# The first layer's feed-forward stage one slot later in a slot-ordered two-layer transformer kernel

## The chip, the cores and the metric

The kernel runs on one core of a Trainium2 chip. The metric is the device time of one execution in microseconds (us). The time before is the median of three runs.

## The reference

Two pre-norm transformer layers act on x of shape (8, 256, 128), 16 heads of 8 features, all in float32:

```python
x = x + attn0(norm(x))   # RoPE, causal; two softmaxes, gated mix, @ Wo.T
x = x + relu(norm(x) @ W1 + b1) @ W2 + b2          # 128 -> 512 -> 128
x = x + attn1(norm(x)*g + b)  # biases, full softmax
x = x + (silu(n @ Wg.T) * (n @ Wu.T)) @ Wd.T       # n = norm(x), 128 -> 384 -> 128
```

## The kernel before

**Phases and slots.** There are 16 phases, i = 0 to 15: first the eight batches of layer 0, then the eight of layer 1. Each phase has 16 slots, one for each head. In slot s, TensorE (PE) first makes the plain scores of head s of the *next* phase (`scores(i + 1, s)`, lines 947 to 951), then the scores of head s of *this* phase with the maximum already subtracted (`shifted(i, s)`, lines 974 to 978). VectorE (DVE) takes the row maxima of the first (lines 774 to 779), ScalarE (ACT) the exponential of the second (line 615). In layer 0 GpSimd (POOL) sets the masked part of two heads' probabilities to zero in each odd slot (`cut`, lines 486 and 489). In slots 6, 10 and 14, and in slot 2 of the next phase (slot 1 behind a phase of layer 1), PE multiplies four heads' probabilities with V (`pv`, line 1000).

**Rings.** Shifted scores alternate between two PSUM banks, so that `shifted(g)` waits for the exponential of slot g - 2. The plain scores have three banks: slot g waits for the maximum of slot g - 3. `pv` for slots 0 to 3 waits for the cuts of slots 1 and 3.

**Everything else rides in the slots.** The dictionary `STEP` says for each step of a batch in which phase (counted from the batch's own) and slot it is issued; `due(L, name, i, s)` is asked in each slot by each engine's program, which is written out in order. So `"xT1": (1, 15)` is issued one phase after the batch's own, in slot 15. An engine's instructions run in exactly that order: a step that waits holds up all behind it.

**The steps around the change**, for batch b of layer 0, are: the output projection is added to x and its statistics taken on DVE (`add_wo`, lines 795 and 710 to 714, slot 11 of phase b + 1); POOL normalises (`norm1`, lines 436 to 443, slot 12); PE transposes the result (`xT1`, line 897) and ACT copies it out (line 660); PE makes the first two blocks of hidden features (`h0`, line 1030), ACT their ReLUs (`relu0`, `relu1`, line 629); then `h1`, `relu2`, `relu3`; then both halves of the second product (`fa` and `f`, line 1043, which sum in one bank); then DVE adds it to x (`add_f`, line 795). `bn2` (the next statistics, slot 13 of phase b + 2) and `norm2` (slot 2 of phase b + 3, POOL) follow.

**The other work in those slots.** Slot 0: PE projects layer 1's V (`v1`, line 1061) and transposes the negated maxima of slots 8 to 15 of the phase at hand (`mr1`, line 957), which needs the maximum made in slot 15 of the phase before. ACT copies both (lines 647, 619). Slot 1: ACT casts (`hi1`, line 674). Slot 4: `oT0` (line 1009), slot 5: `norm_o` (lines 786, 788). POOL: `xb` in slot 4 (line 527), `zg` in slot 6 (line 510); DVE: `z` in slot 7 (line 819); PE: `zT` (line 1016) and `mr0` (line 957) in slot 9, `wo` (line 1022) and `xT2` (line 897) in slot 10.

**Banks.** `xT1`, `h0`, `h1`, `mr0` with `zT`, and `wo` use bank 7 one after the other; each waits until the one before it is emptied. `f`, `xT2`, `qk1`, `mr1` and `oT0` use bank 6. The order of uses is computed from `STEP` by `bank_uses`.

**DMA.** SyncE's queue carries the loads of the stacked operands, the stores to scratch, and the two loads of transposed maxima in each phase (line 369).

Of the kernel before, what the change touches and what calls it, by code (L numbers as in the profile page):

```python
# [40 lines left out]


STEP = ({"oT0": (1, 4), "norm_o": (1, 5), "zg": (1, 6), "z": (1, 7), "zT": (1, 9), "wo": (1, 10), "add_wo": (1, 11),
         "norm1": (1, 12), "xT1": (1, 15), "h0": (2, 1), "relu0": (2, 2), "relu1": (2, 3), "xb": (2, 4), "h1": (2, 5),
         "relu2": (2, 6), "relu3": (2, 7), "fa": (2, 7), "f": (2, 8), "add_f": (2, 9), "bn2": (2, 13), "norm2": (3, 2),
         "xT2": (3, 10), "copy_xT2": (3, 11), "q1": (3, 13), "qk1": (3, 13), "copy_q1": (3, 14), "copy_k1": (3, 14),
         "hi1": (4, 1), "lo1": (4, 10), "v1": (4, 0)},
        {"bv": (0, 10), "oT1": (1, 4), "norm_o": (1, 5), "res": (1, 6), "bn3": (1, 7), "norm3": (1, 8), "xT3": (1, 13), "hi3": (1, 13),
# [1173 lines left out]
```

## Time and profile before

| | |
|---|---|
| Median of three runs | 309.39 us (309.39 to 310.2) |
| The profiled execution's own time | 311.73 us |
| Its span in the profile | 310.0 us |
| Busy, PE / DVE / ACT / POOL | 93% / 80% / 69% / 59% |

The span runs from the first to the last instruction of the core. Busy shares are averages over stages with different limits. The matmuls' ends in the profile are modelled; their starts are used here.

### The profile page before, as it was taken

How to read it: one execution, taken by the hardware profiler on the slowest of the kernel's cores; microseconds unless marked ns; L12 is line 12 of the kernel's file. 1: busy time of each engine (PE TensorE's matmuls, PEld its weight loads, DVE VectorE, ACT ScalarE, POOL GpSimd, SP SyncE). 2: the span in 40 equal slices, each digit the busy share in tenths (PEclk: the TensorE clock that was granted, in tenths of full speed). 3: DMA queues.
4: the chain of work that ended last, by engine and by line, in shares of the span. 5: the costliest groups of instructions: out<-in, count | busy, mean ns of one | idle time of the engine just before them, and what ended most of it. 6: DMA issues, size and time to landing. Idle time of an engine off the chain costs nothing.

```text
span 310.0 us, 8437 instructions
## 1 busy us (share of the span) xinstructions
PE 288.1 (93%) x2833; PEld 206.1 (66%) x2833; DVE 246.9 (80%) x992; ACT 213.2 (69%) x494; POOL 182.2 (59%) x409
## 2 busy tenths in 40 slices
PE   6498898899998999999999999999999999999985
PEld 4375555677676777878687776766666666666564
DVE  7669987687869877686878777679898989896764
ACT  8463784776576868685867768697778767677921
POOL 5475879887785878687778514525455535353210
PEclk9967999999999999999999999999999999999999
DMA  6477436511313121221212010021211101000001
GB/s 188 151 196 176 110 94 178 163 51 56 121 39 103 36 85 54 80 59 41 76 39 60 21 57 26 28 62 29 60 45 52 53 28 44 28 22 1 20 18 35
DMA packets 23691, 21.60 MB, mean 70 GB/s; under 512 B 3712, under 2 KB 20608, under 8 KB 23648
## 3 DMA queue, kind: packets, MB, share of 16 engines
q1 hardware_dynamic: 23648, 21.05, 23.5%
q8 instruction: 23, 0.38, 0.5%
q14 instruction: 20, 0.16, 0.2%
HBM read 13.18 MB, written 7.34 MB: 66 GB/s over the span
## 4 chain that ended last, share of the span: by engine, by line
PE 50%; DVE 22%; POOL 16%; issue 5%; ACT 3%; DMA 2%; SPq 1%; POOLq 0%; ACTq 0%; DVEq 0%
PE bank L1000 11%; DVE NM L779 7%; PE bank L974 5%; PE bank L1043 4%; PE bank L1030 4%; PE bank L950 4%; POOL PB L489 3%; PE bank L951 3%; PE bank L978 3%; POOL XN L443 3%; DVE JUNK L776 3%; PE bank L1089 3%; POOL RS L439 2%; POOL PR L459 2%; DMA xs<-in_x 2%
## 5 line engine op out<-in xcount | busy, mean ns | idle before, releaser
L615 ACT ACTIVATE PB<-bank 128x384 f32<-128x384 f32 (+1 forms) x256 | 134.3, 545 | 47.1 <-PE bank L976 23.6
L779 DVE TENSOR_REDUCE NM<-bank 128x2 f32<-128x512 f32 x128 | 83.8, 683 | 19.7 <-PE bank L951 19.4
L974 PE MATMUL bank<-QS,KS 128*128 128x256 f16 x256 | 69.9, 274 | 3.8 <-ACT PB L615 2.6
L1000 PE MATMUL bank<-PB,VP 128*32 128x256 f32 (+1 forms) x1024 | 61.7, 358 | 0.4 <-ACT PB L615 0.4
L776 DVE CUSTOM_DVE_ANT_0 JUNK<-bank,MSF 128x256 bf16<-128x256 f32 x128 | 53.7, 419 | 0.0
L774 DVE CUSTOM_DVE_ANT_0 JUNK<-bank,MSF 128x128 bf16<-128x128 f32 x128 | 36.3, 284 | 19.5 <-PE bank L948 19.0
L1000 PEld LDWEIGHTS bank<-PB,VP 128*32 128x32 f32 x1024 | 26.8, 109 | 23.2 <-issue 9.7
L489 POOL TENSOR_SCALAR_AFFINE_SELECT PB<-PB 128x512 f32<-128x512 f32 x64 | 41.2, 643 | 0.0
L950 PE MATMUL bank<-KS,QS 96*128 96x256 f16 x128 | 35.2, 275 | 0.4
L948 PE MATMUL bank<-KS,QS 96*128 96x256 f16 x128 | 34.9, 275 | 0.0
L951 PE MATMUL bank<-KS,QS 96*128 96x256 f16 x128 | 34.6, 271 | 0.0
L978 PE MATMUL bank<-QS,KS 128*128 128x256 f16 x128 | 34.3, 271 | 0.0
L974 PEld LDWEIGHTS bank<-QS,KS 128*128 128x128 f16 x256 | 24.6, 96 | 13.6 <-ACT PB L615 10.0
L947 PE MATMUL bank<-KS,QS 96*128 96x128 f16 x128 | 28.7, 225 | 2.6 <-DVE NM L776 2.6
L976 PE MATMUL bank<-QS,KS 128*128 128x128 f16 x128 | 27.8, 217 | 0.0
L486 POOL TENSOR_TENSOR HELD<-EPSC 128x1 f32<-128x1 f32 x64 | 13.1, 205 | 24.5 <-ACT PB L615 24.4
L443 POOL TENSOR_SCALAR XN<-xs,NMN,RS 128x128 f32<-128x128 f32 x54 | 24.5, 463 | 4.8 <-POOL RS L439 4.8
L478 POOL CAST HGL<-HG 128x256 f16<-128x256 f32 x15 | 6.0, 399 | 32.0 <-DVE HG L808 32.0
L897 PE MATMUL bank<-IDF,XN 128*128 128x128 f32 x64 | 13.3, 291 | 7.1 <-DVE XN L721 4.5
L911 PE MATMUL bank<-XT,W 128*128 128x256 f32 x64 | 19.0, 434 | 0.9 <-ACT XT L572 0.6
L439 POOL TENSOR_TENSOR RS<-VE,EPSC 128x2 f32<-128x2 f32 x27 | 19.4, 718 | 0.0
L950 PEld LDWEIGHTS bank<-KS,QS 96*128 96x128 f16 x128 | 12.4, 97 | 10.0 <-DVE NM L779 6.3
(104 smaller groups left out, 590.7 us busy)
## 6 DMA issues: line engine op xcount, KB each, us to landing
scr<-PR SPq DMA_DIRECT2D x16, 256.0 KB, 2.6
QS<-scr SPq DMA_DIRECT2D x16, 128.0 KB, 2.6
QS<-scr SPq DMA_DIRECT2D x32, 64.0 KB, 2.8
KS<-scr SPq DMA_DIRECT2D x32, 64.0 KB, 2.7
KS<-scr SPq DMA_DIRECT2D x16, 128.0 KB, 2.9
scr<-PR SPq DMA_DIRECT2D x16, 128.0 KB, 1.9
out_x<-xs SPq DMA_DIRECT2D x8, 128.0 KB, 2.0
W<-in_w SPq DMA_DIRECT2D x1, 576.0 KB, 4.8
```

The costliest lines, as they stand in the source:

```text
L443: ins = pool.tensor_scalar(XN[n][p][:, t], xs[:, b * TPB + t], NMN[:, n, p, t:t + 1], RS[:, n, p, t:t + 1], ALU.add, ALU.mult)
L489: pool.affine_select(out=pr, in_=pr, compare_op=ALU.is_ge, fill=0.0, base=0, pattern=[[0, 4], [1, P]], channel_multiplier=-1).then_inc(s_c ...
L615: act.activation(PB[:, s % RING, 0:n], scored(i, s)[:, 0:n], ACT.Exp).then_inc(s_e, 1)
L774: dve.tensor_tensor_reduce(JUNK[:, g % 3, 0], o[:, 0:P], MSF[:, 1], -1.0, 3e38, ALU.add, ALU.min, accum_out=m[:, s, 0:1])
L776: dve.tensor_tensor_reduce(JUNK[:, g % 3, 1:3], o[:, P:3 * P].rearrange("q (n k) -> q n k", n=2), MSF[:, :], -1.0, 3e38, ALU.add, ALU.min, ...
L779: dve.tensor_reduce(m[:, s, 0:2], o[:, :].rearrange("q (n k) -> q n k", n=2), AX.X, ALU.max, negate=True).then_inc(s_mx, 1)
L948: ins = pe.matmul(o[:, P:3 * P], q[:, P:2 * P], k[:, :], start=True, stop=True)
L950: pe.matmul(o[:, 0:S], q[:, 0:P], k[:, :], start=True, stop=True)
L951: ins = pe.matmul(o[:, S:2 * S], q[:, P:2 * P], k[:, :], start=True, stop=True)
L974: pe.matmul(o[:, 0:S], k[:, 0:P], q[:, :], start=True, stop=True)
L978: ins = pe.matmul(o[:, S:2 * S], k[:, P:2 * P], q[:, :], start=True, stop=True)
L1000: ins = pe.matmul(o, v, pr, start=(g % 2 == 0 and kt == 0), stop=True, skip_group_check=True)
```

## The change

The transposes of the first layer's FFN input move from slot 15 of phase b + 1 to slot 0 of phase b + 2, and the products, ReLUs, both halves of the output and the add each move one slot on. `xb`, `bn2`, `norm1` and `norm2` stay, and no instruction is added or removed.

```diff
-         "norm1": (1, 12), "xT1": (1, 15), "h0": (2, 1), "relu0": (2, 2), "relu1": (2, 3), "xb": (2, 4), "h1": (2, 5),
-         "relu2": (2, 6), "relu3": (2, 7), "fa": (2, 7), "f": (2, 8), "add_f": (2, 9), "bn2": (2, 13), "norm2": (3, 2),
+         "norm1": (1, 12), "xT1": (2, 0), "h0": (2, 2), "relu0": (2, 3), "relu1": (2, 4), "xb": (2, 4), "h1": (2, 6),
+         "relu2": (2, 7), "relu3": (2, 8), "fa": (2, 8), "f": (2, 9), "add_f": (2, 10), "bn2": (2, 13), "norm2": (3, 2),
```

## Rows read from the trace of the kernel before

**Rows 1.** The page: busy time and share of each engine.

```profile
PE 288.1 (93%) x2833; PEld 206.1 (66%) x2833; DVE 246.9 (80%) x992; ACT 213.2 (69%) x494; POOL 182.2 (59%) x409
```

**Rows 2.** Waits, whole span: waiter, releaser, us in total, times, longest.

```profile
PE bank L897 <- POOL XN L443: 2.1, 5, 0.8
```

**Rows 3.** Stretches: from:to, length, busy of each engine, clock, DMA share, GB/s.

```profile
118.40:135.30 16.90, 16.36 (x178) 12.66 (x176) 12.67 (x81) 12.21 (x31) 12.82 (x32) 1.00 0.21 64
```

**Rows 4.** The same view, slots 11 to 15 of phase 5.

```profile
129.96:134.61 4.65, 4.11 (x45) 2.84 (x43) 4.52 (x34) 3.72 (x10) 3.37 (x10) 1.00 0.21 62
```

**Rows 5.** Timeline, phase 5 into 6: start us, us, engine, line, operation.

```profile
133.95 0.44 PE L897 MATMUL bank<-IDF,XN 128*128 128x128 f32 x2 [0.33 <-POOL XN L443]
...
134.22 0.22 PE L947 MATMUL bank<-KS,QS 96*128 96x128 f16 x1
...
134.53 0.08 DVE L776 DVE_READ_ACCUMULATOR2_ANT NM<- 128x1 f32 x1
...
134.56 0.66 PE L1061 MATMUL bank<-W,XT 128*128 128x128 f32 x4
...
135.05 0.27 PE L957 MATMUL bank<-IDF,NM 128*16 128x128 f32 x1
...
135.16 0.22 PE L947 MATMUL bank<-KS,QS 96*128 96x128 f16 x1
```

**Rows 6.** Timeline, phase 3, slot 0.

```profile
83.21 0.08 DVE L776 DVE_READ_ACCUMULATOR2_ANT NM<- 128x1 f32 x1
...
83.44 0.27 PE L957 MATMUL bank<-IDF,NM 128*16 128x128 f32 x1 [0.36 <-DVE NM L776]
```

**Rows 7.** Timeline, phase 6, slots 3 to 5: `shifted`, exponentials.

```profile
137.81 0.27 PE L974 MATMUL bank<-QS,KS 128*128 128x256 f16 x1
...
138.18 0.49 ACT L615 ACTIVATE PB<-bank 128x384 f32<-128x384 f32 x1
...
138.92 0.88 ACT L615 ACTIVATE PB<-bank 128x384 f32<-128x384 f32 x2
```

**Rows 8.** Timeline, phase 5, slots 11 and 13: the two-bank ring.

```profile
130.26 0.48 ACT L615 ACTIVATE PB<-bank 128x384 f32<-128x384 f32 x1
...
130.80 0.28 PE L974 MATMUL bank<-QS,KS 128*128 128x256 f16 x1 [0.20 <-ACT PB L615]
```

**Rows 9.** Timeline of PE, phase 6, slots 5 to 9.

```profile
138.92 0.27 PE L974 MATMUL bank<-QS,KS 128*128 128x256 f16 x1
...
139.18 1.10 PE L1030 MATMUL bank<-XT,W 128*128 128x256 f32 x4
140.12 0.22 PE L947 MATMUL bank<-KS,QS 96*128 96x128 f16 x1
...
140.54 0.86 PE L1000 MATMUL bank<-PB,VP 128*32 128x256 f32 x16
141.33 0.23 PE L947 MATMUL bank<-KS,QS 96*128 96x128 f16 x1
```

**Rows 10.** Timeline of POOL, phase 6, slots 2 and 3.

```profile
138.26 0.88 POOL L443 TENSOR_SCALAR XN<-xs,NMN,RS 128x128 f32<-128x128 f32 x2 [0.18 <-POOL RS L439]
...
139.24 0.64 POOL L489 TENSOR_SCALAR_AFFINE_SELECT PB<-PB 128x512 f32<-128x512 f32 x1
```

**Rows 11.** Timeline, phase 2: DVE `z`, PE `zT`; then `z` of phase 6.

```profile
73.37 0.97 DVE L819 SCALAR_TENSOR_TENSOR Z<-ZG,Y 128x256 f32<-128x256 f32 x1 [1.35 <-POOL ZG L510]
...
74.49 0.41 PE L1016 MATMUL bank<-IDF,Z 128*128 128x128 f32 x2 [0.43 <-DVE Z L819]
...
142.27 0.42 DVE L819 SCALAR_TENSOR_TENSOR Z<-ZG,Y 128x256 f32<-128x256 f32 x1
```

**Rows 12.** Timeline, phase 3: ACT's exponential of slot 8; PE `zT`; DVE's differences.

```profile
92.41 0.52 ACT L615 ACTIVATE PB<-bank 128x384 f32<-128x384 f32 x1
...
92.89 0.39 PE L1016 MATMUL bank<-IDF,Z 128*128 128x128 f32 x2
...
93.82 1.77 DVE L741 TENSOR_TENSOR PR<-QR,PR 128x512 f16<-128x512 f32 x2
```

## The prediction, made before the changed kernel ran

> **What bounds the kernel.** I read the page first, then the waits, then the phases as stretches, and last the timeline of one steady phase on each engine. PE is busy 93% of the span, DVE 80%, and nothing else comes near [rows 1]. Apart from its matmuls, then, only PE's waits can give time, and a new wait of PE costs its full length where PE sets the pace. The wait that the change is about stands in the list of waits: the transposes of `xT1` (line 897) wait for POOL's normalised input, 2.1 us in five waits, the longest 0.8 [rows 2]. The steady period, shown here for phase 5, is 16.9 us, with the clock at its full level [rows 3]. The reader is to see two things there. From slot 11 to slot 15 DVE is busy 4.52 of 4.65 us: it sets the pace, and PE's wait for POOL lies inside that stretch [rows 4]. From slot 0 to slot 10 PE sets the pace, and what costs is a point where a short slot leaves PE ahead of ACT or POOL.
>
> **Part 1, the transposes leave slot 15.** In phase 5 they start at 133.95, after a wait of 0.33 for POOL, and the scores of slot 0 follow at 134.22: work of 0.27 [rows 5]. In slot 0, `mr1` needs DVE's last maximum, which ends at 134.53 + 0.08 = 134.61; before, it ran at 135.05, so only 0.44 lies between [rows 5]. Where it really waited, PE came 0.15 behind DVE: 83.44, with the maximum read out at 83.21 + 0.08 = 83.29 [rows 6]. So `mr1` now runs at 134.76 at the earliest. Behind it come its own 0.11 (135.05 to 135.16) and the transposes' 0.27, and the scores of slot 1 are at 135.14 instead of 135.16 [rows 5]. The gain is nothing: the wait moves from POOL to DVE, and the transposes now stand behind it instead of inside it. Bounds: if DVE came earlier by all of the 0.33, the gain would be 0.3; where `mr1` waits already, as in phase 3, it is a loss of 0.27. The copy out on ACT (line 660) has until slot 2 and is covered. POOL's and SyncE's orders don't change; the loads of transposed maxima are issued at most some tenths earlier or later, for a use eight slots on, so I put them at 0.
>
> **Part 2, `h0` from slot 1 to slot 2.** It now follows `pv`. Both lie before slot 3, so the sum stays: 0.
>
> **Part 3, `h1` from slot 5 to slot 6.** It is 0.94 of PE (139.18 to 140.12) and was what lay between slot 5 and slot 6 [rows 9]. Without it two things come late. First, ACT: `relu0` and `relu1` now stand in slots 3 and 4, and an exponential with a ReLU behind it takes 0.74 (138.18 to 138.92) [rows 7]. The exponential of slot 3 stays at 138.18, that of slot 4 at 138.92. `shifted` runs 0.54 behind the start of the exponential two slots earlier where it waits for it [rows 8], so that of slot 6 is at 139.46; a slot with nothing but scores takes PE 0.34 (134.22 to 134.56) [rows 5], so PE alone would be there at 138.92 + 0.34 = 139.26 [rows 9]. Second, POOL: `pv` in slot 6 needs the cut of slot 3, which stands behind `norm2` on POOL and ends at 139.24 + 0.64 = 139.88 [rows 10]. Before, `pv` ran at 140.54 with 0.66 to spare [rows 9]. Now it runs at about 139.93, 0.61 earlier, with 0.94 of `h1` still to come: the scores of slot 7 come at 141.33 - 0.61 + 0.94 = 141.66, a loss of 0.33. I take 0.3. Bounds: 0 if both releasers came earlier by as much, 0.94 if neither `pv` nor the scores moved up at all.
>
> **Part 4, `relu3` from slot 7 to 8, `f` from 8 to 9.** Slot 9's `zT` and `mr0` need bank 7, which `relu3` empties. By part 3 the shifted scores of slot 7 come 0.18 behind its plain ones, at 141.84 (slot 5's, at 138.92, stand 0.26 ahead of `h1` [rows 9], of the 0.34 of a whole slot), and their exponential at 142.21: it follows by 0.37, as 138.18 follows 137.81 [rows 7]. With 0.74 for that pair [rows 7], slot 8's starts at 142.95, and `relu3` runs from 143.33 to 143.80. `fa` has as many columns as `h1`, so PE passes slot 7 in 0.34 and slot 8 in 0.34 + 0.94 = 1.28, and would be at `zT`, 0.2 into slot 9, at about 143.66. It waits until about 143.86, a loss of 0.2; bounds 0 and 0.4. `f` follows in slot 9 with nothing to wait for, and `add_f` on DVE in slot 10 has until `xT2` on PE, which there comes behind `pv` and `wo`: 0.
>
> **A steady phase** loses 0.3 + 0.2 = 0.5. That holds for phases 4 to 7, 2.0 in all. Phase 8 has no cuts, since its probabilities are layer 1's; I give it 0.3. Phase 9 has no `zT`: 0.1.
>
> **Phase 2.** `z` is late there: it ends at 73.37 + 0.97 = 74.34, and `zT` waits 0.43 for it [rows 11]. Half of the output product (0.94, as `h1`) stood ahead of that wait, in slot 8, and now stands behind it. POOL's chain up to `zg` starts from the exponential of slot 3, which moves back by at most 0.5 by the squares that ACT has in slots 1 and 15. So the loss is 0.94 to 1.44; I take 1.2. `z` takes 0.97 here and 0.42 in phase 6, where it starts while POOL waits [rows 11]. The Trainium skill, SBUF — State Buffer, section "SBUF: two separate sides", says that a DVE operation with two SBUF inputs and a GpSimd operation take a shared port pair in turn, as an exclusive lock. By that rule `z` could stretch in the steady phases too, if the cut of slot 7 starts ahead of it; that would add up to 0.1 to each of them; the trace agrees in phase 2 (0.97) and shows nothing of it in phase 6 (0.42).
>
> **Phase 3.** The boundary costs 0.27 [rows 6]. In slot 7 ACT has two casts for batch 7 behind its ReLU, and the exponential of slot 8 starts only at 92.41 [rows 12]. `relu3` stood ahead of the casts; now it stands behind that exponential, from about 92.8 to 93.3, and `zT`, before at 92.89, runs at 93.33. With the moved half product behind it, slot 10 is late by 0.44 + 0.94 = 1.4. DVE gives some of it back: its two differences keep it busy until 95.59 [rows 12], so that its next maxima were late already, by about 0.5. Loss: 0.9 + 0.3 = 1.2; bounds 0.3 and 1.7.
>
> **The sum** is 4 × 0.5 + 0.3 + 0.1 + 1.2 + 1.2 = 4.8. Behind phase 9 nothing changes, and PE sets the pace there, so it stays. The profiled execution took 311.73 us with a span of 310.0, 2.3 above the median of the runs. Against its own time the sum gives 316.5; carried over to the median, 309.39 + 4.8 = 314.2 us.
>
> **Rivals.**
> *(A) Faster: the wait for POOL was worth its length.* If DVE's run in slots 11 to 15 isn't what `mr1` waits for, the 2.1 us [rows 2] come back, and with no loss behind them that gives 307.3. For it: the wait is in the list. Against it: DVE is busy 97% of that stretch [rows 4]. It decides if `mr1` in slot 0 starts before 134.6 of the old time. Chance 0.05.
> *(B) No change.* ACT's and POOL's lateness in slots 5 to 9 is absorbed because PE's short slots start them earlier too; only the boundary is shifted: 309.4 ± 0.9. For it: each loss is a few tenths. Against it: the cut of slot 3 hangs on POOL's queue from slot 1 on, which no edit starts earlier. Chance 0.10.
> *(C) Slower by the steady phases alone*, phases 2 and 3 absorbed by DVE's late work: 2.4, so 311.8. Chance 0.2.
> *(D) The forecast*, 312.8 to 315.8: chance 0.62. The last 0.03 is for more lateness in phases 2 and 3 than reckoned, above 316.
>
> **The range** runs from 311.0, which takes in (C) with its steady loss at 0.25 a phase, to 316.0. What this measurement can tell from no change is about 0.3%, 0.93 us. Faster than that: 0.05; within it: 0.10; slower: 0.85.
>
> **What would show it.** In the profile after: no wait of PE for POOL at `xT1`, but one for DVE at `mr1` (line 957) in slot 0 of phases 5 to 8; a start of `pv` in slot 6 right behind the cut of slot 3; `zT` right behind `relu3`; a period of about 17.4 us in phases 5 to 7; phases 2 and 3 later by 1.2 each. The prediction is wrong if the steady period is at or under 16.95, which would mean that DVE's run starts earlier than slot 11 lets it, or that the order in slots 5 to 9 lets PE through.

## The result, and the profile after

The changed kernel takes 314.29 us (median of six runs, 313.76 to 315.48) against 309.92 us for the kernel before, run beside it. The ratio is 1.0145, with a 95% interval of 1.0123 to 1.0166. The forecast was 314.2 us, slower. One execution in the runs below, the first profiled one of the output half alone, took 682.65 us, over twice the others; it is left out.

The page, busy time by engine, answers to [rows 1]:

```profile
PE 288.2 (92%) x2833; PEld 204.4 (66%) x2833; DVE 245.4 (79%) x992; ACT 211.1 (68%) x494; POOL 182.1 (58%) x409
```

The work is the same, 288.2 against 288.1 us on PE. The profiled execution of after took 313.76 us with a span of 311.9, only 1.9 more than before's span. The two executions start differently, though: the first shifted scores of phase 1 (line 974) stand at 46.68 before and at 43.86 after, 2.8 earlier in a stretch of the program that the change doesn't touch. From there to phase 15 the new kernel loses 4.7. So spans of single executions don't compare here, and I take the shifted scores of phase 1, slot 0, as the common zero.

The waits of PE by its matmuls, whole span, columns as in [rows 2]:

```profile
PE bank L957 <- DVE NM L776: 2.1, 6, 1.0
...
PE bank L1016 <- DVE Z L819: 1.2, 1, 1.2
PE bank L1016 <- ACT HR L629: 1.1, 1, 1.1
...
PE bank L1000 <- POOL PB L489: 0.4, 1, 0.4
```

The wait of `xT1` for POOL (2.1) is gone from the list. In its place stand 2.1 of `mr1` for DVE (0.4 before), a longer wait of `zT` for `z` in phase 2 (1.2, 0.43 before), and new waits of `zT` for `relu3` (line 629, in phase 3) and of `pv` for the cut (in phase 4). Shorter waits don't stand in the list; they are read from the timelines below. A steady period, the same work as in [rows 3]:

```profile
118.40:135.85 17.45, 16.79 (x179) 12.74 (x177) 12.46 (x83) 11.87 (x32) 12.90 (x32) 1.00 0.23 65
```

The clock is at its full level here too. The two stretches, 16.90 and 17.45, are cut by hand; from the first shifted scores (line 974) of phase 5 to those of phase 6 it is 16.96 before and 17.41 after. Timeline of after, phase 5 into 6, answering to [rows 5]:

```profile
134.46 0.66 PE L1061 MATMUL bank<-W,XT 128*128 128x128 f32 x4
135.34 0.28 PE L957 MATMUL bank<-IDF,NM 128*16 128x128 f32 x1 [0.22 <-DVE NM L776]
135.45 0.40 PE L897 MATMUL bank<-IDF,XN 128*128 128x128 f32 x2
135.68 0.22 PE L947 MATMUL bank<-KS,QS 96*128 96x128 f16 x1
```

and DVE beside it:

```profile
135.20 0.08 DVE L776 DVE_READ_ACCUMULATOR2_ANT NM<- 128x1 f32 x1
```

DVE's last maximum is read out at 135.28 and `mr1` runs 0.06 behind it; the transposes stand behind that, and the scores of slot 1 come 0.40 behind the maximum's end. Before, it was 135.16 - 134.61 = 0.55 [rows 5]. The gain is 0.15.

Phase 6, slots 5 to 9 on PE, answering to [rows 9]:

```profile
139.48 0.27 PE L974 MATMUL bank<-QS,KS 128*128 128x256 f16 x1
...
140.02 0.28 PE L974 MATMUL bank<-QS,KS 128*128 128x256 f16 x1
...
140.48 0.86 PE L1000 MATMUL bank<-PB,VP 128*32 128x256 f32 x16
141.26 1.13 PE L1030 MATMUL bank<-XT,W 128*128 128x256 f32 x4
...
144.01 0.27 PE L974 MATMUL bank<-QS,KS 128*128 128x256 f16 x1
...
144.42 0.44 PE L1016 MATMUL bank<-IDF,Z 128*128 128x128 f32 x2
```

and who releases it, POOL's cut and then ACT's pair and its last ReLU:

```profile
139.79 0.64 POOL L489 TENSOR_SCALAR_AFFINE_SELECT PB<-PB 128x512 f32<-128x512 f32 x1
```

```profile
139.47 0.49 ACT L615 ACTIVATE PB<-bank 128x384 f32<-128x384 f32 x1
...
143.88 0.49 ACT L629 ACTIVATE HR<-bank,SM 128x256 f32<-128x256 f32 x1
```

The shifted scores of slot 6 are at 140.02, 0.54 behind those of slot 5 where 0.34 of work lies between, and 0.55 behind the exponential of slot 4 (139.47). `pv` starts at 140.48, 0.05 behind the cut's end (140.43). `zT` starts at 144.42, 0.05 behind `relu3`'s end (144.37).

The gain and loss by phase, worked out from the timelines: the start of the shifted scores after minus before, as the phase adds to it. "Boundary" is from slot 10 of the phase before to slot 3, "middle" from slot 3 to slot 10.

```
phase             2     3     4     5     6     7     8     9
boundary       +0.5  +0.2  -0.6  -0.1  -0.1  -0.2  +0.1  -0.1
middle         +0.9  +1.2  +0.9  +0.6  +0.6  +0.2  +0.6  +0.2
sum            +1.4  +1.4  +0.3  +0.4  +0.5  +0.1  +0.6  +0.1
```

The sum, before rounding, is 4.7.

### The profile page after: what moved, and what is told of

The parts are those of the page before. It is cut to its first block, busy times and chain, and to the rows that moved or that the text cites. A ratio compares the mean times of both kernels' runs of the same rounds, so it can differ in the third digit from the quotient of the medians.

```text
span 311.9 us, 8437 instructions
## 1 busy us (share of the span) xinstructions
PE 288.2 (92%) x2833; PEld 204.4 (66%) x2833; DVE 245.4 (79%) x992; ACT 211.1 (68%) x494; POOL 182.1 (58%) x409
## 4 chain that ended last, share of the span: by engine, by line
PE 44%; DVE 27%; POOL 14%; ACT 7%; issue 6%; DMA 2%; SPq 0%; POOLq 0%; ACTq 0%; DVEq 0%
PE bank L1000 11%; DVE NM L779 8%; PE bank L974 4%; PE bank L1030 4%; DVE JUNK L776 4%; POOL PB L489 4%; PE bank L950 3%; ACT PB L615 3%; PE bank L951 3%; PE bank L1043 3%; PE bank L978 3%; PE bank L1089 3%; DVE JUNK L774 2%; POOL PR L459 2%; DVE HG L808 2%
## 5 line engine op out<-in xcount | busy, mean ns | idle before, releaser
L911 PE MATMUL bank<-XT,W 128*128 128x256 f32 x64 | 17.6, 408 | 1.0 <-ACT XT L572 0.6
L950 PEld LDWEIGHTS bank<-KS,QS 96*128 96x128 f16 x128 | 12.4, 97 | 9.0 <-DVE NM L779 5.3
L947 PEld LDWEIGHTS bank<-KS,QS 96*128 96x128 f16 x128 | 12.5, 98 | 8.5 <-issue 4.0
```

What stands on the lines that cost most here:

```text
L947: pe.matmul(o[:, 0:P], q[:, 0:P], k[:, 0:P], start=True, stop=True)
L950: pe.matmul(o[:, 0:S], q[:, 0:P], k[:, :], start=True, stop=True)
```

## The experiments

Each time is a median beside runs of the kernel before on the same chip. "By slots" is the time from the shifted scores of phase 1, slot 0, to those of phase 15, slot 0, in the kernel's own profile, less the same in the profile of before; it leaves out the start of the program, which differs from execution to execution. The changed kernel itself is +4.7 by slots and +1.45% by time.

### The transposes alone

```diff
-"xT1": (1, 15)
+"xT1": (2, 0)
```

> Only the transposes (`xT1`) go to slot 0; h0 stays in slot 1 and all else where it was. My theory (the transposes' wait is inside DVE's run): no gain at the boundary of two phases, at most 0.1 a phase, and a new wait, since h0 in slot 1 now stands right behind ACT's copy of the transposes, which comes third in ACT's slot 0: about 0.4 in each of phases 2 to 8. Sum +1.5 to +3 us against before. Rival (the wait for POOL was worth its length): faster by 1 to 2 us.

Measured: 313.26 us against 310.13, ratio 1.0094 (1.0068 to 1.0121), +3.7 by slots. Its timeline at the boundary of phases 4 and 5:

```profile
118.60 0.28 PE L957 MATMUL bank<-IDF,NM 128*16 128x128 f32 x1 [0.22 <-DVE NM L776]
118.71 0.40 PE L897 MATMUL bank<-IDF,XN 128*128 128x128 f32 x2
...
119.84 0.89 PE L1030 MATMUL bank<-XT,W 128*128 128x256 f32 x3 [0.40 <-ACT XT L660]
```

Both waits are there: `mr1` for DVE, and `h0` for the copy that now comes third in ACT's slot 0. The part of the change that was to give time costs two thirds of the loss by time (0.94% of 1.45%) if it is made alone. The rival (A) is refuted. By slots it is above what I had expected, since phase 2 alone lost 1.2.

### All but the transposes

```diff
-"xT1": (2, 0)
+"xT1": (1, 15)
```

(against the changed kernel)

> The changed kernel with `xT1` back in slot 15 of the phase before. My theory: the boundary is neutral, so nearly the whole loss stays: +4.0 to +5.0 us against before, within 0.7 of the changed kernel. Rival (what hurts is that the transposes stand behind DVE's last maximum): under +2 us.

Measured: 314.31 us against 310.13, ratio 1.0125 (1.0099 to 1.0151), +5.0 by slots, 0.3 more than the changed kernel. Nearly the whole loss is in the rest of the change. Once `h0` has moved too, the copy is in time, and the transposes' own move gains 0.15 to 0.2 at each boundary of phases 5 to 7 and 0.3 in all by slots; the medians don't resolve that. Phase 2's boundary loses the same 0.5 as in the changed kernel, with the transposes where they were before.

### The output half alone

```diff
-"fa": (2, 7), "f": (2, 8), "add_f": (2, 9)
+"fa": (2, 8), "f": (2, 9), "add_f": (2, 10)
```

(against the kernel before; run twice, the second time for its profile)

> Only fa, f and add_f go one slot on; the transposes, h0, h1 and all four ReLUs stay. My theory: phase 2 loses the cover of the wait for z (0.9), the steady phases lose nothing because relu3 still empties the bank a slot earlier, phase 3 loses at most 0.4. Sum +0.9 to +1.4 us. Rival (the later product and add themselves hurt, through xT2 waiting for add_f's bank in slot 10): +0.3 or more in each phase, +2.5 us or more.

> The kernel of e3 again, for its profile: only fa, f and add_f one slot on. It measured no difference where I had reckoned with +0.9 to +1.4 us. If my theory of phase 2 holds after all, slot 10 of phase 2 is 0.9 late and something later gives it back; if it fell, slot 10 of phase 2 stands where it did.

Measured: 309.93 us, ratio 1.0002 (0.9973 to 1.0030), and 310.82 us, ratio 1.0006 (0.9983 to 1.0029): no difference. By slots it is +0.4. The expectation for phase 2 held and that for the sum didn't: slot 10 of phase 2 is 0.9 late, as reckoned, but phase 3 takes back 0.2 and the boundary to phase 4 another 0.5. Phases 4 to 7 gain 0.05 each, and phase 8 loses 0.3. The list of its waits, whole span:

```profile
PE bank L897 <- POOL XN L443: 1.7, 5, 0.3
PE bank L1016 <- DVE Z L819: 1.4, 1, 1.4
```

The longest wait of `xT1` for POOL fell from 0.8 [rows 2] to 0.3. It stood in slot 15 of phase 3. My reading is that DVE, which was late in slot 11 of that phase anyway, is less late now relative to PE, and so POOL is too: a late PE in front of a late DVE costs little.

### `relu3` back in slot 7

```diff
-"relu3": (2, 8)
+"relu3": (2, 7)
```

(against the changed kernel)

> The changed kernel with relu3 in slot 7, behind relu2, and so in front of ACT's casts in phase 3 and a slot ahead of zT. My theory: the wait of zT for the bank goes, 0.2 to 0.4 in each of phases 4 to 9 and about 1.2 in phase 3: 2.0 to 2.7 us less than the changed kernel, so about +2.2 us against before. Rival (ACT is merely late, and the wait comes back as a wait for exponentials): under 1 us less than the changed kernel.

Measured: 312.82 us against 310.13, ratio 1.0069 (1.0043 to 1.0095), +1.7 by slots: 3.0 less than the changed kernel by slots, 2.4 by the two ratios. One ReLU's place is worth more than half of the loss. Phase 3's middle goes from +1.2 to -0.1, those of phases 5 and 6 from +0.6 to +0.3, which is the 0.2 of the wait and 0.06 that the moved half product gives by itself (the output half alone shows the same 0.06).

### `norm2` in slot 0, against the changed kernel

```diff
-"norm2": (3, 2)
+"norm2": (3, 0)
```

> The changed kernel with POOL's norm2 in slot 0 instead of slot 2, in front of the cuts of slots 1 and 3. My theory (the product in slot 6 waits for the cut of slot 3, which stands behind norm2): that wait goes in phases 4 to 6, 0.2 to 0.45 each, so 0.6 to 1.0 us less than the changed kernel. Rival (only ACT's exponential of slot 4 holds PE there): no change, within 0.3 us.

Measured: 313.03 us against 310.44, ratio 1.0104 (1.0076 to 1.0133), +3.9 by slots, 0.85 less than the changed kernel. In phase 6 the period between the shifted scores of slots 6 and 7 falls from 2.38 to 2.19, which is the work of `pv`, `h1` and the scores; those of slots 5 and 6 stay 0.55 apart. So the cut and the exponential of slot 4 are two waits, one behind the other. Of the 0.33 that phases 5 and 6 lost between slots 3 and 7, 0.18 was the cut; 0.15 stays.

### `bn2` in slot 10, against the kernel before, and with the transposes alone

```diff
-"bn2": (2, 13)
+"bn2": (2, 10)
```

> The kernel before with bn2 (0.7 us of DVE) moved out of DVE's run in slots 11 to 15 into DVE's gap in slot 10. My theory: in the kernel before, mr1 in slot 0 had 0.44 to spare behind DVE, since POOL's wait in slot 15 came first, so there is little to gain: 0 to 0.5 us. Rival (DVE's run sets the period before as well): 0.5 or more in each of phases 4 to 8, 2.5 us or more faster.

> Only the transposes in slot 0, as in the first run, and bn2 in slot 10. My theory: with DVE's run shorter, mr1 no longer waits for it, and moving the transposes out of slot 15 is worth its 0.3 a phase: 1.2 to 2.0 us less than the transposes alone. Rival (the wait for DVE isn't what took the gain): same as the transposes alone, within 0.4.

Measured for the first: 310.74 us against 310.44, ratio 1.0019 (1.0001 to 1.0037), +0.8 by slots, where I had expected a gain of 0 to 0.5. From phase 4 on every slot stands exactly as before. The net loss is all in phase 3 (0.4 lost in slot 13 of phase 2 comes back in slot 15): 0.2 in slot 8 and 0.65 in slots 14 and 15. There DVE is late from its two differences (line 741, 1.77) in slot 10, and `bn2` now stands between them and `add_wo`, which starts 0.65 later against slot 10; I had not reckoned with that. In the steady phases the edit shows that DVE's run did not set the pace before. Its timeline at the end of phase 5:

```profile
134.19 0.44 PE L897 MATMUL bank<-IDF,XN 128*128 128x128 f32 x2 [0.33 <-POOL XN L443]
...
134.30 0.08 DVE L776 DVE_READ_ACCUMULATOR2_ANT NM<- 128x1 f32 x1
...
134.83 0.29 DVE L774 CUSTOM_DVE_ANT_0 JUNK<-bank,MSF 128x128 bf16<-128x128 f32 x1 [0.45 <-PE bank L948]
...
135.29 0.27 PE L957 MATMUL bank<-IDF,NM 128*16 128x128 f32 x1
```

DVE is done with slot 15's maximum 0.91 ahead of `mr1` (135.29 - 134.38) instead of 0.44, and then waits for PE; PE's own wait for POOL is 0.33 as before. POOL's input comes from `add_wo` in slot 11, ahead of the place that `bn2` left.

Measured for the second: 311.91 us, ratio 1.0056 (1.0035 to 1.0078), +2.2 by slots, 1.4 less than the transposes alone. The wait of `mr1` for DVE is gone in phases 4 to 8, but the boundaries of phases 5 to 8 are then only level with the kernel before: `h0` in slot 1 still waits 0.3 to 0.4 for the copy in each. So DVE's run took part of the transposes' gain, and the place of `h0` the rest; the next run has both out of the way.

### `bn2` in slot 10, against the changed kernel

> The changed kernel with bn2 in slot 10. My theory: mr1 in slot 0 stops waiting for DVE, 0.3 in each of phases 4 to 8 and 0.5 in phase 3: 1.5 to 2.2 us less than the changed kernel. Rival: the wait moves on to POOL or ACT (the exponential of slot 1, the cut of slot 3), and less than 0.5 us comes back.

Measured: 313.16 us against 310.44, ratio 1.0087 (1.0063 to 1.0110), +3.0 by slots, 1.7 less than the changed kernel. Here `h0` is in slot 2, and each boundary of phases 5 to 7 is 0.5 shorter than in the kernel before (0.1 to 0.2 in the changed kernel). So the wait for POOL was worth its 0.3 and a little more, once neither DVE's last maximum nor the copy came behind it. Phase 3 loses 0.4 more than in the changed kernel, where I had expected it to gain 0.5.

### The three waits removed together

`relu3` in slot 7, `norm2` in slot 0 and `bn2` in slot 10, against the changed kernel.

> The changed kernel with relu3 in slot 7, norm2 in slot 0 and bn2 in slot 10, the three single edits of before together. If the three waits are separate, their gains add up, by the slots' times in the profiles 3.0 + 0.85 + 1.7 of the 4.7 lost: 0.5 to 1.5 us faster than before. Rival (they hide each other, or one of them brings a wait that the next one uncovers): between 0 and +2 us.

Measured: 309.61 us against 310.14, ratio 0.9969 (0.9948 to 0.9989), -0.9 by slots. The single gains were 3.0, 0.85 and 1.7, together 5.6; all at once they give 4.7 + 0.9, the same 5.6. The waits are separate and add up. With them gone, the whole is a small gain over the kernel before. Phase 2 still loses 1.5 in it. `norm2` in slot 0 was not tried on the kernel before, so how much of the gain is the move's own isn't fully shown.

### The transposes first in slot 0

On PE the block of `xT1` moves in front of `mr1`, and on ACT its copy in front of the two other copies; in `STEP` only `xT1` moves.

```diff
-"xT1": (1, 15)
+"xT1": (2, 0)
...
+                    for b in due(0, "xT1", i, s):
+                        pe.wait_ge(s_xn[1], b + 1)
+                        norm_t("xT1", 1, b)
                     if s == m1_slot(i) and 0 <= i < NPH:
                         m = into("mr1", i)
```

> The transposes alone in slot 0, but issued there ahead of v1 and mr1 on TensorE, and their copy ahead of the two other copies on ScalarE; all else as before the change. My theory (what takes the gain is the place behind mr1, which waits for DVE, and the third place in ScalarE's slot 0): both new waits go. PE does slot 0's scores while POOL finishes and reaches mr1 just as DVE's last maximum ends: 0.3 to 0.4 us gained in each of phases 4 to 8, nothing in phases 2, 3 and 9: 1.0 to 2.0 us faster than before, 4 to 5 us faster than the transposes alone. Rival (slot 0 itself is too late for the product in slot 1): slower than before by 1 us or more.

Measured: 309.35 us against 310.14, ratio 0.9971 (0.9951 to 0.9992), -0.8 by slots. Its timeline into phase 6:

```profile
132.63 0.44 PE L897 MATMUL bank<-IDF,XN 128*128 128x128 f32 x2
132.91 0.61 PE L1061 MATMUL bank<-W,XT 128*128 128x128 f32 x4
133.36 0.27 PE L957 MATMUL bank<-IDF,NM 128*16 128x128 f32 x1
133.47 0.22 PE L947 MATMUL bank<-KS,QS 96*128 96x128 f16 x1
```

```profile
133.21 0.08 DVE L776 DVE_READ_ACCUMULATOR2_ANT NM<- 128x1 f32 x1
```

`mr1` comes 0.07 behind DVE's end (133.29) with the transposes already done, and the scores of slot 1 come 0.18 behind it, against 0.55 in the kernel before. Each of phases 4 to 7 gains 0.4; phase 8 gains 0.3. Phase 2 loses 1.1, mostly in one wait of `h0` for the copy, which is line 647 in this kernel:

```profile
PE bank L1030 <- ACT XT L647: 0.9, 1, 0.9
```

### The same, from batch 2 on

The kernel of the last section, with one more line changed:

```diff
...
+STEP_OF = {(0, 0): {"xT1": (1, 15)}, (0, 1): {"xT1": (1, 15)},
...
```

> As the run with the transposes first in slot 0, but batches 0 and 1 keep them in slot 15, since by the slots' times phase 2 lost 1.1 us there (ScalarE has a square to do in that place) and phases 4 to 8 gained. My theory: phases 2 and 3 stand as in the kernel before, phases 4 to 8 keep their 0.3 to 0.4 each: 1.5 to 2.1 us faster than before. Rival (the gain of phases 4 to 8 only gives back what phase 2 lost): no difference, within 0.5 us.

Measured: 308.25 us against 309.95, ratio 0.9945 (0.9915 to 0.9974), -2.0 by slots. It is the best of the kernels, 0.55% faster than the one before.

## Why the prediction was right, step by step

- **What bounds the kernel.** PE sets the pace in slots 0 to 10: moving what it waited for there (`relu3`, `norm2`) gave the waits back. That DVE sets it in slots 11 to 15 was wrong for the kernel before. With 0.7 us taken out of that run its steady phases did not get shorter at all. A busy share of 97% was no proof: what PE waited for was POOL's input, and DVE's last maximum stood 0.44 ahead of `mr1`. Part 1 came out right all the same, because it reckoned with that 0.44 and not with the pace. That the path from `add_wo` over `norm1` sets the end of the phase is what the waits say; it was not tried by itself.
- **Part 1** (boundary 0): the four steady phases gained 0.1, 0.1, 0.2 and, in phase 4, 0.6. The 0.15 that I gave `mr1` behind DVE's end is 0.06 in phase 6. Phase 4's larger gain is the lateness given back behind phase 3, which I had booked in phase 3; the output half alone shows 0.5 of it at the same place, with the transposes unmoved.
- **Part 2** (`h0`, 0): not exact. At phase 2's boundary 0.5 is lost; by the timelines PE made `h0` while ACT did its square, and now waits, as slot 1 holds nothing else. All but the transposes loses the same 0.5 there and the output half alone nothing, so it lies with `h0`, `h1` and the ReLUs; `h0` was not tried by itself. I had that 0.5 only as the upper end of phase 2's term.
- **Part 3** (0.3): 0.33 in phases 5 and 6, 0.6 in phase 4, 0.1 in phase 7. The two causes, the exponential of slot 4 and the cut, are seen in the timeline; the cut's share (0.2, and 0.5 in phase 4) is shown by moving `norm2`, the exponential's 0.15 is only read. Phase 7 was 17.44 long before (slot 10 to slot 10), not 16.96, has slots longer by 0.05 and no wait for the cut; I had priced it like the others.
- **Part 4** (0.2): 0.2 in phases 4 to 6, 0.1 in phase 7, and `relu3` back in slot 7 takes it away. The step on `f` "with nothing to wait for" was wrong for phase 9, where `f` itself waited for `relu3`, 0.3, hidden in a total of 0.1.
- **Phases 4 to 9:** 2.4 reckoned, 1.9 measured, with 0.3, 0.4, 0.5, 0.1 for phases 4 to 7, 0.6 instead of 0.3 for phase 8, and 0.1 for phase 9.
- **Phase 2** (1.2): 1.4. The wait of `zT` for `z` is 1.2, where it was 0.43, with the half product behind it; the output half alone repeats it (1.4 of wait, slot 10 late by 0.9).
- **Phase 3** (1.2): 1.4. `zT` waited 1.1 for `relu3`, behind the casts. The 0.5 that DVE gives back came at the next boundary.
- **The sum** was 4.8; by slots it is 4.7, by time 4.4. Part of that agreement is luck: phases 2 and 3 were 0.4 too low and phases 4 to 9 0.5 too high. That 314.2 meets the 314.29 measured is luck too: the kernel before took 309.92 beside it, 0.5 more than the 309.39 that I had added the sum to.
- **`z` and POOL.** The rule of the Trainium skill (SBUF — State Buffer, "SBUF: two separate sides") would have let `z` stretch in the steady phases. The trace of after shows `z` at 0.98 in phase 2, beside a cut, and 0.42 in phases 4 to 7; the rule alone was not tested here. I had overlooked phase 8, where `z` took 1.26 before and 1.06 after, beside POOL's subtraction (line 535). Before, in phase 8:

```profile
177.42 1.16 POOL L535 TENSOR_TENSOR PR<-QR,PR 128x512 f16<-128x512 f32 x1
...
177.59 1.26 DVE L819 SCALAR_TENSOR_TENSOR Z<-ZG,Y 128x256 f32<-128x256 f32 x1
```

  In all four cases `z` ended 0.28 behind the end of POOL's instruction, whatever its own length, which fits a wait for that end. In phase 4 of the kernel before it was the other way round: `z` took 0.42, and the cut beside it 0.85 instead of 0.64.
- **Rivals.** (A) is refuted by the transposes alone; that the time could be had is shown by the two last kernels, with the transposes in front of `mr1` instead of behind it. (B) fell with `pv`'s wait for the cut. (C) fell in the changed kernel, where phases 2 and 3 lost 2.8 of the 4.7, though 0.6 came back behind them; in the output half alone 0.6 of the late 0.9 came back in that way.

What stays open: why moving `bn2` costs 0.2 in slot 8 of phase 3, how the exponential's 0.15 in slots 5 and 6 could be had back, and which of `z` and the cut is the one to wait when they meet; none was tried.

## What to carry to other kernels

A wait in a list was worth its length here only where the next wait behind it was already over: before moving a step out of a wait, look up what else the engine will wait for in the next slot, and put the step in front of that wait, not behind it. In a program of fixed slots a long matmul between two short slots is also cover for the engines that feed the second one; move it, and the exponential, the cut or the bank release that it covered shows. An engine that is busy 97% of a stretch need not set its pace: take something out of the stretch and see. Reckon each affected phase by itself, with its own late engines, since the irregular ones (here two of eight) carried more than half of the loss.

## What the runs showed that I had not expected

The start of the same program differs by 2.8 us between two profiled executions (first shifted scores of phase 1 at 46.68 and 43.86), while from there on the phases that an edit doesn't touch repeat within 0.04 over their whole length. So a difference of 0.4 us can be read off one trace by aligning it behind the start, where medians of six to twelve runs have an interval of 0.2 to 0.3% (0.6 to 0.9 us) to either side.
